# Value products in pairs of steps, a ring of twelve tiles of exponentials, and other orders at the start and at the bridge of a macaron block

## What is computed

```
x = x + 0.5 * ffn(layernorm(x))     # gate and up (256 to 2048), gelu(gate) * up, down (2048 to 256), 4-bit weights with scales
x = x + attention(layernorm(x))     # causal softmax over 2048 keys, head size 16
x = x + 0.5 * ffn(layernorm(x))     # the same weights
```

## Time and profile before

| | |
|---|---|
| median of 3 runs | 1105.14 us (1104.61 to 1107.93) |
| the profiled execution | 1102.31 us |
| its span, first to last instruction | 1100.6 us |
| mean granted clock of TensorE | 0.995 of full speed |
| PE busy | 1051.6 us, 96% of the span |
| DVE busy | 692.0 us, 63% |
| ACT busy | 562.9 us, 51% |

### The profile page before, as it was taken

How to read it: one execution, slowest core, us unless ns; L and a number is a source line. 1 busy time by engine, 2 the same in 40 slices (tenths; PEclk the granted TensorE clock), 3 DMA queues, 4 the chain that set the end, 5 groups by cost and what they waited for, 6 DMA issues and landing times.

```text
span 1100.6 us, 16821 instructions
## 1 busy us (share of the span) xinstructions
PE 1051.6 (96%) x6240; PEld 673.0 (61%) x6240; DVE 692.0 (63%) x1589; ACT 562.9 (51%) x1028; POOL 95.6 (9%) x337
## 2 busy tenths in 40 slices
PE   4999999999998789999999999999999999999998
PEld 3888888887776423332223333333448888888887
DVE  5986544446566488899898988985424434343333
ACT  5664443442344646666667777777663334233222
POOL 0000000000002035221101102111110000000000
PEclk9999999999999989999999999999999999999999
DMA  7001040042140651212013012010000000000000
GB/s 198 2 1 34 1 134 1 10 139 55 27 129 14 168 122 35 69 50 54 1 34 73 16 39 54 2 39 2 1 1 1 1 20 1 1 20 1 20 1 20
DMA packets 85155, 43.75 MB, mean 40 GB/s; under 512 B 47954, under 2 KB 85074, under 8 KB 85074
## 3 DMA queue, kind: packets, MB, share of 16 engines
q1 hardware_dynamic: 85074, 42.69, 14.9%
HBM read 25.63 MB, written 16.78 MB: 39 GB/s over the span
## 4 chain that ended last, share of the span: by engine, by line
PE 79%; DVE 11%; ACT 2%; issue 2%; DMA 2%; SPq 2%; POOL 1%; ACTq 0%; POOLq 0%; DVEq 0%
PE psum L882 16%; PE psum L663 15%; PE psum L815 9%; PE psum L756 9%; PE psum L774 8%; PE psum L899 8%; PE psum L678 8%; DVE attn_part_max L1365 8%; PE psum L710 2%; PE psum L858 1%; PE psum L123 1%; DMA qk_rows<-qkv_parts 1%; ACT attn_prob L1180 1%; PE psum L722 1%; DMA attn_q<-attn_max_rows 1%
## 5 line engine op out<-in xcount | busy, mean ns | idle before, releaser
L1175 ACT ACTIVATE attn_prob<-psum 128x512 f32<-128x512 f32 (+3 forms) x548 | 257.0, 537 | 138.4 <-PE psum L756 135.7
L1365 DVE TENSOR_REDUCE attn_part_max<-psum 128x1 f32<-128x512 f32 x384 | 236.1, 683 | 13.7 <-PE psum L774 12.7
L663 PE MATMUL psum<-ffn_xt,all_w_hi 128*128 128x512 f32 x512 | 166.0, 406 | 0.0
L815 PE MATMUL psum<-attn_prob,attn_vals 128*32 128x512 f32 (+3 forms) x1280 | 151.2, 545 | 2.1 <-POOL attn_prob L585 0.8
L1368 DVE CUSTOM_DVE_ANT_0 attn_junk<-psum,attn_mask 128x128 bf16<-128x128 f32 (+3 forms) x256 | 114.6, 488 | 41.9 <-PE psum L774 41.1
L1471 DVE TENSOR_TENSOR ffn_act_out<-ffn_act_out,psum 128x512 f32<-128x512 f32 x64 | 44.1, 689 | 111.9 <-ACT ffn_act_out L1216 111.7
L1216 ACT ACTIVATE ffn_act_out<-psum 128x512 f32<-128x512 f32 x64 | 38.3, 598 | 130.1 <-PE psum L882 130.1
L663 PEld LDWEIGHTS psum<-ffn_xt,all_w_hi 128*128 128x128 f32 x512 | 91.5, 189 | 17.2
L678 PE MATMUL psum<-all_w_hi,ffn_inner 128*128 128x256 f32 x512 | 101.7, 283 | 0.1
L663 PE MATMUL psum<-ffn_xt,all_w_lo 128*128 128x512 f32 x256 | 101.6, 397 | 0.0
L899 PE MATMUL psum<-all_w_hi,ffn_inner 128*128 128x256 f32 x512 | 100.3, 280 | 0.1
(11 more groups left out here) (148 smaller groups left out, 1618.6 us busy)
## 6 DMA issues: line engine op xcount, KB each, us to landing
qk_rows<-qkv_parts SPq DMA_DIRECT2D x16, 384.0 KB, 2.5
qk_rows<-qkv_parts SPq DMA_DIRECT2D x16, 256.0 KB, 3.0
attn_q_early<-qk_rows SPq DMA_DIRECT2D x8, 384.0 KB, 3.5
attn_k_early<-qk_rows SPq DMA_DIRECT2D x8, 384.0 KB, 4.7
attn_vals<-v_rows SPq DMA_DIRECT2D x48, 64.0 KB, 3.8
attn_k<-qk_rows SPq DMA_DIRECT2D x8, 384.0 KB, 3.7
attn_q<-qk_rows SPq DMA_DIRECT2D x8, 384.0 KB, 3.6
attn_k_late<-qk_rows SPq DMA_DIRECT2D x8, 384.0 KB, 3.5
```

Of the source, the lines that this page charges most:

```text
L663: last = nc.tensor.matmul(psum[:, 2 * m + q % 2, :], w_part[a][:, 3 * g + m, pl, o:o + P], xt[:, b % 2, c, pl, :], start=(n == 0), stop=(n ...
L815: last = nc.tensor.matmul(psum[32 * hd:32 * hd + 32, O0, at:BT], vals[:, r % KSLOTS * SUB + kb % SUB, VALUES_AT[hd]:VALUES_AT[hd] + 32], p ...
L1175: nc.scalar.activation(prob[:, n % PRING, at:BT], psum[:, score_bank(n), at:BT], ACT.Exp).then_inc(s["exp"], 1)
L1365: nc.vector.tensor_reduce(to, psum[:, bank, :], AX.X, ALU.max).then_inc(s["max_read"], 1)
```

## The change

Four things change, all else stays.

1. From step 14 on the value products of two steps are issued together behind every even step: `weigh(d - 2)` and `weigh(d - 1)`. The exponentials get a ring of twelve tiles (`PRING_2`) from step 12 on: `prob` and four tiles `prob_late`, reached by `weights(n)`. To make room there is one `o_sb` in place of two, and the weights `Wo` (`raw_o`) are loaded at step 132 into memory that is free by then, counted in `loaded_w`.
2. In the bridge, maxima are due in steps 4 to 6 only, in banks 2 and 7 by turns; those of step 7 use the ring of three. DVE's order within these steps is changed.
3. At the start, the first 128 columns of jobs 0 and 1 are scaled and split ahead of the rest (`first_scale`, `first_high`, `first_low`), the products of q = 0 wait for these alone, and the table for the square root is loaded ahead of the first copy.
4. Waits follow: ACT's step d waits for steps up to d - 3 to be weighed, `gather(0)` waits for the reads of the bridge's maxima, and so on.

```diff
+PRING_2 = 12
+PAIRS_FROM = 12
...
-            BRIDGE = {(4, 0): 1, (4, 2): 1, (5, 0): 1, (5, 2): 1, (5, 3): 1, (6, 0): 1, (6, 1): 1, (6, 3): 1,
-                      (7, 0): 1, (7, 1): 1, (7, 2): 1, (7, 3): 1}
+            BRIDGE = {(4, 0): 2, (5, 0): 1, (5, 1): 1, (5, 3): 1, (6, 0): 1, (6, 1): 1, (6, 3): 1}
...
-                return 2 if n < N_EARLY + N_BRIDGE else M0 + n % MBANKS
+                return (2, X0)[n % 2] if n < N_EARLY + N_BRIDGE else M0 + n % MBANKS
...
-                o_sb = tb("o_sb", [P, 2, BT], F32)
+                o_sb = tb("o_sb", [P, BT], F32)
+                prob_late = tb("prob_late", [P, PRING_2 - PRING, BT], F32)
...
+                def weights(n, count=1):
+                    k = n % PRING if n < 4 * PAIRS_FROM else (n - 4 * PAIRS_FROM) % PRING_2
+                    return prob[:, k:k + count] if k < PRING else prob_late[:, k - PRING:k - PRING + count]
...
-                        sp.dma_start(raw_o[:, :, :], Wo.rearrange("(hh p) c -> p hh c", p=P)).then_inc(s["loaded_o"], 16)
...
+                            if d == begin[14]:
+                                sp.wait_ge(s["weighted"], d)
+                                sp.dma_start(raw_o[:, :, :], Wo.rearrange("(hh p) c -> p hh c", p=P)).then_inc(s["loaded_w"], 16)
...
-                            elif m == 1:
+                            elif k == 1:
                                 pe.wait_ge(s["weight"], 2)
+                                pe.wait_ge(s["turned"], 2)
-                            if b == 0 and q % GT == 0:
+                            if k == 0:
+                                pe.wait_ge(s["first_w_lo"], m + 1)
+                            elif b == 0 and (q == 1 or q % GT == 0):
                                 pe.wait_ge(s["w_lo"], 3 * g + m + 1)
...
-                            if d >= 1:
+                            if 1 <= d <= PAIRS_FROM:
+                                weigh(d - 1)
+                            elif d > PAIRS_FROM and d % 2 == 0:
+                                weigh(d - 2)
                                 weigh(d - 1)
...
+                        weigh(NS - 2)
                         weigh(NS - 1)
...
+                        nc.scalar.activation(deviation[:, TT - 1:TT], nc.const_aps.tensor(1.0, [P, 1], F32), ACT.Sqrt)
+                        take_byte(0)
+                        widen(0)
                         root(0)
+                        take_turned(0)
+                        take_byte(1)
+                        widen(1)
+                        take_turned(1)
+                        first_high(0)
                         split(0)
+                        first_high(1)
                         take_byte(2)
                         widen(2)
+                        weight_high(0)
+                        weight_high(1)
...
-                            if d >= 2:
-                                act.wait_ge(s["weighted"], d - 1)
+                            if d == PAIRS_FROM + 2:
+                                for u in range(2):
+                                    act.wait_ge(s[f"part_out{u}"], 96 * NB)
+                            elif d >= 2:
+                                act.wait_ge(s["weighted"], d - 1 if d < PAIRS_FROM + 2 else d - 2)
...
                         variance(0)
+                        norm(0)
                         decode(0)
-                        norm(0)
+                        first_scale(0)
+                        decode(1)
+                        first_scale(1)
+                        split(0)
+                        first_low(0)
+                        first_low(1)
                         scale_weight(0)
-                        decode(1)
+                        scale_weight(1)
                         weight_low(0)
-                        split(0)
-                        scale_weight(1)
                         weight_low(1)
```

More of the change, by code:

```diff
@@ L310, in program @@
                     ot_even = tensors(before_keys, "proj")("ot_even", [P, 2, PL, BT], F32R)
+                    with ExitStack() as before_xb:
+                        raw_o = tensors(before_xb, "proj")("raw_o", [P, 2, H], F32)
                     xb2 = tensors(before_keys, "ffn2")("xb", [P, SUB, H], F32)
@@ L767, in maxima @@
                                 pe.wait_ge(s["max_read"], n - MBANKS + 1)
[L768 to L772, removed]
+                            elif n >= N_EARLY + N_BRIDGE:
+                                pe.wait_ge(s["max_read"], N_EARLY + N_BRIDGE)
+                                pe.wait_ge(s["full"], NU * NB)
+                                pe.wait_ge(s["v"], SUB * NB)
+                            elif n >= N_EARLY + 2:
+                                pe.wait_ge(s["max_read"], n - 1)
+                            elif n == N_EARLY + 1:
+                                pe.wait_ge(s["x_free"], turn_use[EARLY - 1] + 1)
                             cols = BT if c < qt else P * (i + 1)
@@ L1036, in weight_high, with first_high @@
                             act.wait_ge(s["weight"], n + 1)
-                            nc.scalar.activation(w_hi[:, n, :, :], weight[:, n % 2, :, :], ACT.Copy).then_inc(s["w_hi"], 1)
+                            cols = slice(P if n < 2 else 0, GT * P)
+                            nc.scalar.activation(w_hi[:, n, :, cols], weight[:, n % 2, :, cols], ACT.Copy).then_inc(s["w_hi"], 1)
+                        def first_high(n):
+                            act.wait_ge(s["first_weight"], n + 1)
+                            nc.scalar.activation(w_hi[:, n, :, 0:P], weight[:, n, :, 0:P], ACT.Copy).then_inc(s["first_w_hi"], 1)
                         def root(use):
@@ L1104, in copy_out @@
                             act.wait_ge(s["weighted"], begin[g + 1])
-                            if g >= 2:
-                                act.wait_ge(s["x_full"], gather_use[g - 2] + 1)
-                            nc.scalar.activation(o_sb[:, g % 2, :], psum[:, O0, :], ACT.Copy).then_inc(s["o_copied"], 1)
+                            if g >= 1:
+                                act.wait_ge(s["x_full"], gather_use[g - 1] + 1)
+                            nc.scalar.activation(o_sb[:, :], psum[:, O0, :], ACT.Copy).then_inc(s["o_copied"], 1)
                         def copy_max(g):
@@ L1484, in last_block @@
                             if d == 4:
+                                maxima(mine[1])
                                 first_rest(u)
-                                maxima(mine[1])
                                 take_rows(i)
@@ L1615, in build_program @@
         NORM = "aggr var std rstd xb "
-        W_SEMS = "ident turned_s wide turned_c byte turned weight w_hi w_lo step value scales0 scales1 scales2 "
+        W_SEMS = "first_weight first_w_hi first_w_lo ident turned_s wide turned_c byte turned weight w_hi w_lo step value scales0 scales1 scales2 "
         CODE_SEMS = " ".join(f"codes{n}" for n in range(3 * NG))
         F1_SEMS = NORM + "stats xt_turned gu product inner_lo down added xt_hi xt_lo gelu inner_hi x0 x1 x2 x3 "
-        Q_SEMS = ("newton loaded loaded_o wt wfull wt_hi wt_lo unit v_sum v bias_q full part_1 part_2 part_3 rest "
+        Q_SEMS = ("newton loaded loaded_o loaded_w wt wfull wt_hi wt_lo unit v_sum v bias_q full part_1 part_2 part_3 rest "
                   "part_out0 part_out1 v_out0 v_out1 v_out2 v_out3 ")
```

50 lines of the change are left out of this document (27 added, 23 removed).

## The result

The changed kernel takes 1126.81 us (median of 4 runs, 1124.48 to 1129.0), beside 1104.88 us (4 runs) of the kernel before on the same chip. The ratio is 1.019, with a 95% interval of 1.016 to 1.022: 2% slower. The forecast was 1118, its range 1093 to 1132. In the profiled executions the span grew from 1100.6 to 1122.7 us, by 22.1.

A forecast was written before the change was run, and what follows sets the result against it. PE looked busy nearly throughout, but a PE-DVE loop through three banks bound full steps: 17 + 8 - 4.5 - 1.5 - 4.5 = plus 14.5 on 1102.3, 1116.8 profiled; median forecast 1118 us, range 1093 to 1132.

The forecast's parts named there:

- a loop: Attention: DVE waits for PE behind each pair; two full-width steps take 7.28 us with 10 maxima, 6.05 with 8.
- Rival (a): PE alone counts, DVE and ACT hide their losses, every saved switch shows: 1079 to 1082 us, chance 0.17.
- (b): The loop holds, but backlog carried between pairs of unlike steps takes half of it: 1104 to 1106 us, chance 0.10.
- (d): The ring doesn't free ACT, which stalls about 1 us in each pair: 1180 us, chance 0.03.
- (c): Loop at its upper bound and the early gains lost: 1128 to 1130 us, chance 0.13.
- The pair: Value products on PE: second product 0.90 us, 1.98 us together against 2.16 for two single ones, 0.18 us less.
- The body: 61 pair periods between the ends of steps 14 and 136: plus 17 us, bounds minus 11 and plus 22.
- The periods with a gather: Twelve pair periods in the body holding `gather` and `normalise`, 0.5 us more on DVE: plus 0.75 each, 9 us.
- the 23 periods set at 0: Body pairs with short value products covered by three banks, or narrow maxima where ACT's score banks bind: 0.
- The tail: Four score banks, ACT waits: 5.15 us per two full-width steps against 4.25; plus 8, bounds minus 2 and plus 11.
- Start, bridge and clock: Early gains: start minus 4.5 us, bridge minus 4.5, less time at half clock with shorter waits minus 1.5.
- the bridge's 4.5: Steps 4 to 7: 3 us from PE's waits for masked maxima, 1.5 from Wo's load leaving SP's queue; bounds 0, minus 7.

The follow-up runs named there:

- the short reads: Changed kernel with VectorE reading only 128 columns of each maximum product in the attention: 1072.9 us with pairs, 1074.13 us with one value product at every step.
- pairs apart: Changed kernel with the two value products in the even step separated, the first behind the second score, the second at the step's end: 1109.26 us, ratio 1.0056.
- the pairs alone: Kernel before with pairs, ring of twelve, one o_sb and Wo's later load, but its own start and bridge: 1131.33 us, ratio 1.0245.
- start alone: Kernel before with the new start, ring of twelve, one o_sb and Wo's later load; no pairs, its own bridge: 1097.86 us, ratio 0.9945.
- bridge alone: Kernel before with the new bridge, ring of twelve, one o_sb and Wo's later load; no pairs, its own start: 1099.81 us, ratio 0.9969.
- the ring alone: Kernel before with ring of twelve, one o_sb and Wo's later load; no pairs, its own start and bridge: 1100.08 us, ratio 0.9983.

## Why the prediction was right, and where it was off

**Direction and cause: right.** The forecast named a loop: TensorE away for one pair, three banks of maxima that cover less, and VectorE that waits. The 1.1 us of idle time before the first maximum stands in both timelines, the periods are 7.16 and 5.96 where 7.28 and 6.05 were forecast, and the short reads show that the loop is the cause: without it the pairs gain. Rival (a) was the mechanism that is left when VectorE has room: it works, with 8.9 us in the body, but in this kernel VectorE has none. Rivals (b) and (d) are out: the loop took its full price, and ScalarE waits for scores, not for value products. Of (c), 1128 to 1130, the half that says the early gains are given back came partly true.

**The pair: 0.90 for the second product was right** (0.88), and the pair until the next score takes 1.86, under the 1.90 in my sum. That, and reads of 0.607 us where the sum has 0.616, is why both periods came out 0.1 us shorter than forecast. The saving of 0.18 measured 0.2 to 0.25. The Trainium skill ("TensorEngine Tiling (Array Packing)", Key Properties) says that a change of tiling mode drains the engine. The trace with short reads agrees as far as it goes: one change fewer saves 0.24 us; that it is a drain, no trace shows.

**The body: 17 forecast, 19.4 measured** from step 17 on; with the two periods of steps 13 to 17, which the forecast counted in, it is 23.4, over its upper bound of 22 (most of the 4.0 there goes with the clock, see below). From step 17 on two errors partly cancel. The periods with a gather were to cost 0.75 each, 9 in all; the eleven between steps 17 and 135 cost 3.7, and the three with narrow maxima among them nothing, for most of VectorE's 0.5 us of `normalise` fits into the idle time that the pair itself makes: the full-width periods with it take 7.21 and 6.01 us, those without 7.16 and 5.96. On the other side, the 23 periods set at 0 were not free: ten of the eleven pairs with value products of 256 and 128 columns cost 0.35 to 0.43 each, 3.9 together. "Short enough for three banks to cover" was the step that failed: it was said of each value product, and a pair of them with the changes around it is not covered. Eight pairs of 512 and 384 columns cost 0.56 to 0.86 each, 5.1 together, where the sum had 3. The plain 8-maxima pairs cost 0.27, near the 0.3 forecast.

**The tail: 8 forecast, 6.4 measured.** The period was right (5.15 forecast, 5.11 measured, plus 0.86). But only five of the eight full-width pairs cost that much; the other three (odd steps 137, 145 and 147) cost 0.9 together, and why so little is open. The run with pairs apart adds what I had not seen: mostly the uneven steps do it, not the length of the absence.

**Start, bridge and clock: -10.5 forecast, -7.7 by step 13**, and 4.0 of it given back by step 17. The start came 5.4 us sooner, forecast 4.5, with the first gate product at 15.11 in place of 21.50 (forecast 16). The first score behind the row maxima starts at 391.13 in place of 399.01, 7.9 us sooner (forecast 9). The error is in the other two terms. The half clock was to shrink by 1.5 us; it grew. The windows of the changed kernel that lie inside its four early half-clock stretches:

```profile
16.00:19.00 3.00, 3.00 (x10) 2.12 (x9) 2.95 (x5) 2.69 (x5) 0.00 (x0) 0.50 1.11 349
371.50:374.00 2.50, 2.50 (x13) 0.68 (x11) 2.10 (x11) 0.83 (x2) 0.00 (x0) 0.50 1.12 340
392.00:394.50 2.50, 2.50 (x16) 1.05 (x14) 1.90 (x9) 1.97 (x4) 1.04 (x4) 0.50 0.00 0
405.50:411.50 6.00, 6.00 (x29) 2.09 (x27) 3.08 (x11) 3.51 (x6) 0.00 (x0) 0.50 0.01 3
```

and of the kernel before, in its two:

```profile
380.00:383.00 3.00, 3.00 (x14) 0.74 (x12) 1.88 (x7) 0.60 (x1) 0.00 (x0) 0.50 1.07 375
400.50:406.50 6.00, 6.00 (x26) 2.61 (x24) 4.87 (x20) 3.53 (x8) 1.75 (x6) 0.50 0.56 144
```

In full the stretches of the changed kernel last 3.4 us three times and 6.8 once, 17 us at 1.2 GHz up to step 17, against 10 before (3.4 and 6.8). "With shorter waits part may stay at 2.4 GHz" failed: shorter waits on VectorE did not leave fewer. And the bridge's 4.5: 1.5 of it, Wo's load, measured 1.6 by itself at step 11, and the bridge about 2 where I took 3. But in the changed kernel the row maxima's transfer did not come under cover. The chain of the changed kernel, in order of time:

```profile
385.63 5.46 DMA attn_q<-attn_max_rows
...
402.85 2.28 DMA attn_q<-attn_max_rows
...
405.17 0.61 PE psum L769
```

and its waits, 345 to 418 us:

```profile
PE psum L790 <- DVE attn_part_max L1421: 4.1, 4, 2.7
PE psum L769 <- DMA attn_q<-attn_max_rows: 3.6, 2, 2.2
```

The transfer takes 5.46 us as it took 5.85, but TensorE comes to it sooner and waits 3.6 us in all in place of 2.2. What was gained on VectorE's waits (4.9 to 4.1 behind its masked maxima) is lost there: this is the wait that takes the removed one's place. My bridge term named it, and counted it as shrinking.

**What stays open:** the 4.0 us of steps 13 to 17. Two things differ there. The wait before 405.17 is 1.45 us, and the same wait of the kernel before 0.85 (at 412.88): 0.6. And TensorE runs at half the clock from 405.1 to 411.9, where the kernel before has the full clock from step 13 to 17; its stretch of the same length fell ahead of step 13. Half of 6.8 us is 3.4 at most. From the start of step 13's product to that of step 17's, the changed kernel, the pairs alone and the pairs apart, against 12.88 us at clock 1.00 before:

```profile
401.20:418.08 16.88, 14.41 (x77) 4.96 (x73) 11.57 (x36) 8.75 (x18) 4.94 (x13) 0.80 0.08 25
...
411.81:425.88 14.07, 11.60 (x77) 4.11 (x73) 11.16 (x36) 8.11 (x18) 4.97 (x13) 1.00 0.10 31
...
399.28:416.52 17.24, 15.65 (x75) 5.39 (x74) 11.47 (x38) 8.88 (x20) 5.44 (x15) 0.70 0.08 25
```

The pairs alone, without a slow stretch there, lose 1.2 us; with the first pair at step 18 it is 2.2 with 3.4 us of half clock, the changed kernel 4.0 with 6.8, the pairs apart 4.35 with 10.2; the three kernels with single products, full reads and no such stretch (no pairs, start alone, bridge alone) lose at most 0.1, and the ring alone 1.3 with 3.4. So most of the 4.0 goes with the place of the slow stretch, and about 1 us with the pairs. That is one execution of each kernel, read and not varied: no run set the clock. What puts the stretch there stays open.

By terms, against the forecast of plus 14.5: early parts 2.8 less gain, steps 13 to 17 plus 4.0, body from 17 on plus 2.4, tail minus 1.6: 7.6, the distance to 22.1. The measured median is 8.8 above the forecast of 1118. My own sum, 1116.8 and the 2.8 by which the median lay above the profiled execution, makes 1119.6; 1118 does not follow from it.

## What to carry to other kernels

Gathering one engine's small pieces into a longer one saves what the changes cost (0.24 us per pair here) and takes away its service to the others for as long. Before doing it, count how many banks the others have in hand. Here three reads of 0.607 us (1.82) stand against the way from the end of a read to the start of the first read behind the value products: 0.09 to the last maximum product, 0.32 to the value products, their own time, 0.23 to the next maximum product and 0.41 to VectorE. With one value product (1.00) that is 2.05 us and VectorE idles 0.23; with a pair (1.86) it is 2.91 and VectorE idles 1.09. The faster kernel here is the one with everything but the pairs, 1096.6 us against 1103.8 before and 1126.8 changed. Part of a gain ahead of a transfer can go into the wait for it: the changed kernel waited 3.6 us for its row maxima in place of 2.2.

## What the runs showed of the hardware

- Value products of two heads (four matmuls, 32 columns of weights each) take 0.99 us, of four heads 1.00: four quarters cost what two do, so splitting by heads doubles the time.
- A change from the 128-column products to the 32-column ones and back costs 0.24 us, which the records show only as 0.09 before (604.46 to 604.77, less a stride of 0.22); the rest is in the start of the product that follows.
- The granted clock fell to half in stretches of 3.4 to 13.7 us, and what they made together differed between the profiled executions: 10 us ahead of step 17 with the bridge alone, 24 us with the start alone and in the kernel without pairs. In one execution with pairs three fell in the body too, at 1.7 us each (an estimate, half of 3.4).
- In 17 executions of the kernel before on one chip, beside the run with the ring alone, the time goes with the mean granted clock: from 1099.0 us at 0.998 to 1108.5 at 0.986, although the kernel was the same. These 9.5 us are more than the 6.9 that start, bridge and ring gain.
